# Identity from a count and a matmul, first two x tiles ahead of narrow weight columns, turned tiles split beside products: the first stage of an attention-and-experts kernel

## The chip, the core and the metric

The kernel runs on one core of one Trainium2 chip. The metric is the device time of one execution in microseconds; the span of a profiled execution is what its trace covers. Engine names are those of the profile: PE is TensorE (PEld its weight loads), DVE VectorE, ACT ScalarE, POOL GpSimd, SP SyncE (SPq its queue of DMA issues).

## What is computed

x is 2048 tokens of 512 features. All arithmetic is float32.

```python
xn = layernorm(x)                                   # over the 512 features, eps 1e-5
s  = latent attention(xn)                           # c_Q = xn W_DQ', c_KV = xn W_DKV', 16 heads of 128 + 64 rotary, causal
w  = top-2 of softmax(xn router_w') over 8 experts
g  = silu(xn weight' + 2 * sum_e w_e (xn A_e') B_e) # rank 16 per expert
return x + s * g
```

## The kernel before

Three programs run one after the other, each a block with a program for every engine: `prepare` (projections of the normalised tokens, to about 151 us of the trace), `attend` (scores, softmax and values, to about 1244 us) and `combine`. The change is in `prepare` alone, and in its first group.

`prepare` takes the 16 tiles of 128 tokens in four groups of four. For a tile, DVE works out mean and variance (L482, L486), ACT the root (L402), DVE the inverse and the normalised tile `xn` (L491, L497). PE turns `xn` by four transposes against the identity `ident` into PSUM (`turn_x`, L310; `turn_ps` has two banks, so a turn waits until DVE has used the tile two before it). ACT rounds it to the high half `xt_h` (L417) and DVE subtracts to get the low half `xt_l` (L504). A float32 product is made as three products of such halves, and the weights are split the same way: ACT `w_h` (L407), DVE `w_l` (L509). The four chunks `w_stage[:, c, :]` hold 128 of the 512 features each, with 1032 columns: 512 for the experts' base, then 128 for the low-rank factors, 8 for the router, 128, 128 and 128 for keys/values, queries and rotary keys.

For a group PE then makes, in this order: for each tile a product with 264 columns (L335, 12 matmuls; ACT copies part of it to `value_out`, L429, DVE takes two parts, L525 and L526; `work_ps` has two banks, so a product waits until DVE has read the one two before it); three products over the four tiles together (L345, 12 matmuls of 512 columns each; in the first group `absorb`, L298, stands after the first of them); the base product (L372, the first to use the 512 wide columns); and the low-rank part (L383 to L385). In the first group PE begins with four turns and nothing runs before all constants are there: PE and ACT wait for the semaphore `constants`, which POOL raises with its memsets and masks. POOL makes `ident` by a memset and an `affine_select`. All order is written out by hand, and every wait is a count on a semaphore.

## Time and profile before

| | us |
|---|---|
| median of 3 runs | 1454.61 (1453.51 to 1456.13) |
| the profiled execution | 1453.58 |
| its span | 1452.1 |
| PE busy | 1378.6 |
| DVE busy | 1141.7 |
| ACT busy | 781.3 |

The span is 1.5 us shorter than the time of the same execution. Busy times of the engines overlap. A timeline row gives the start, the duration from the first instruction's start to the last one's end, and in brackets how long the engine sat idle before it and what ended that.

### The profile page before, as it was taken

To read this page: it belongs to the slowest core of one execution; us is meant where nothing else is said; L and a number is where in the kernel's file an instruction comes from. 1 tells how busy PE (TensorE), PEld (TensorE's weight loads), DVE (VectorE), ACT (ScalarE), POOL (GpSimd) and SP (SyncE) were. 2 spreads that over 40 slices of the span, in tenths; PEclk is the share of its full clock that TensorE was granted. 3 is DMA by queue.
4 is the path that set the end of the run, shared out by engine and by line. 5 is a ranking of instruction groups with operands and counts; after the bars stand their busy time and mean duration, and the time that the engine had idled before them with its cause. 6 is when DMAs were issued, how large, how long until landed. Compare 5 with 4: busy or idle time off the path is not lost. (4 is left out here: it accounts for less than half of the span.)

```text
span 1452.1 us, 27828 instructions
## 1 busy us (share of the span) xinstructions
PE 1378.6 (95%) x9808; PEld 1133.0 (78%) x9808; DVE 1141.7 (79%) x1322; ACT 781.3 (54%) x854; POOL 112.6 (8%) x150
## 2 busy tenths in 40 slices
PE   5999689999999999999999999999999799599998
PEld 5888567778778888888889888887788688278887
DVE  5666378888888898989888898888788598576764
ACT  3322367666666666666666665666556466332221
POOL 0000111101101101010010100100000000112121
PEclk9999899999999999999999999999999999899999
DMA  6422665535424424242251421422412522345562
GB/s 265 134 90 85 187 187 153 168 130 157 120 89 148 123 85 124 84 126 83 58 152 58 123 87 61 136 74 56 129 54 83 189 57 58 117 132 161 167 181 87
DMA packets 111949, 172.77 MB, mean 119 GB/s; under 512 B 9224, under 2 KB 68904, under 8 KB 109096
## 3 DMA queue, kind: packets, MB, share of 16 engines
q1 hardware_dynamic: 97528, 111.10, 24.8%
q0 software_dynamic: 13552, 59.60, 14.0%
q10 hardware_dynamic: 832, 1.57, 0.5%
q8 instruction: 22, 0.36, 0.1%
q14 instruction: 15, 0.12, 0.0%
HBM read 123.75 MB, written 48.50 MB: 119 GB/s over the span
## 5 line engine op out<-in xcount | busy, mean ns | idle before, releaser
L1093 ACT CAST prob_h<-prob 128x1024 fp32r<-128x1024 f32 (+1 forms) x288 | 289.7, 1006 | 230.4 <-DVE prob L1177 183.1
L946 PE MATMUL score_ps<-q_h,key_slot 64*128 64x512 f32 x1792 | 360.8, 394 | 14.7 <-DMA key_slot<-keys 14.5
L1087 ACT ACTIVATE prob<-score_ps 128x1024 f32<-128x1024 f32 (+1 forms) x288 | 281.8, 978 | 168.0 <-PE score_ps L946 119.0
L1195 DVE TENSOR_TENSOR prob_l<-prob,prob_h 128x1024 fp32r<-128x1024 f32 (+1 forms) x288 | 335.9, 1166 | 39.7 <-ACT prob_h L1093 38.2
L968 PE MATMUL out_ps<-prob_h,value_slot 64*128 64x512 f32 (+1 forms) x1792 | 341.5, 375 | 0.2
L1190 DVE TENSOR_TENSOR total<-total,prob 128x1024 f32<-128x1024 f32 (+1 forms) x256 | 294.9, 1152 | 0.0
L1177 DVE TENSOR_SCALAR prob<-prob 128x1024 f32<-128x1024 f32 x224 | 155.2, 693 | 84.8 <-ACT prob L1087 84.6
L946 PEld LDWEIGHTS score_ps<-q_h,key_slot 64*128 64x128 f32 x1792 | 173.8, 185 | 52.8 <-DMA key_slot<-keys 10.8
L968 PEld LDWEIGHTS out_ps<-prob_h,value_slot 64*128 64x128 f32 x1792 | 173.7, 185 | 33.6 <-DVE prob_l L1195 2.3
L946 PE MATMUL score_ps<-q_l,key_slot 64*128 64x512 f32 x896 | 179.0, 391 | 0.0
L946 PE MATMUL score_ps<-rot_hh,key_slot 64*128 64x512 f32 x896 | 178.9, 390 | 0.0
L968 PE MATMUL out_ps<-prob_l,value_slot 64*128 64x512 f32 (+1 forms) x896 | 172.3, 376 | 0.0
L1391 ACT CAST rows_h<-rows 128x1024 fp32r<-128x1024 f32 x32 | 33.7, 1053 | 128.6 <-DVE rows L1423 127.2
L1376 PE MATMUL sum_ps<-merged_h,rows_h 128*128 128x512 f32 x256 | 100.0, 391 | 0.0
L946 PEld LDWEIGHTS score_ps<-rot_hh,key_slot 64*128 64x128 f32 x896 | 86.7, 184 | 16.9
L1378 PE MATMUL sum_ps<-merged_h,rows_l 128*128 128x512 f32 x256 | 99.6, 389 | 0.0
L1377 PE MATMUL sum_ps<-merged_l,rows_h 128*128 128x512 f32 x256 | 99.6, 389 | 0.0
L968 PEld LDWEIGHTS out_ps<-prob_l,value_slot 64*128 64x128 f32 x896 | 86.9, 185 | 16.1
L946 PEld LDWEIGHTS score_ps<-q_l,key_slot 64*128 64x128 f32 x896 | 86.8, 185 | 12.8
L946 PE MATMUL score_ps<-rot_l,key_slot 64*128 64x512 f32 x448 | 89.4, 390 | 0.0
L1182 DVE SCALAR_TENSOR_TENSOR prob<-prob,causal 128x1024 f32<-128x1024 f32 (+1 forms) x64 | 61.1, 954 | 17.3 <-ACT prob L1087 16.9
L1423 DVE TENSOR_TENSOR rows<-rows,scale 128x1024 f32<-128x1024 f32 x32 | 39.5, 1271 | 31.2 <-POOL scale L1358 31.2
(192 smaller groups left out, 1979.9 us busy)
## 6 DMA issues: line engine op xcount, KB each, us to landing
key_slot<-keys SPq DMA_DIRECT2D x144, 256.0 KB, 2.7
value_slot<-values SPq DMA_DIRECT2D x144, 128.0 KB, 2.0
rows<-heads_rows SPq DMA_DIRECT2D x32, 512.0 KB, 5.8
rot_hh<-turned POOLq DMA_DIRECT2D x30, 512.0 KB, 6.0
heads_rows<-head_rows POOLq DMA_DIRECT2D x15, 1024.0 KB, 10.0
turned<-rot_hl POOLq DMA_DIRECT2D x14, 1024.0 KB, 4.6
rot_l<-turned POOLq DMA_DIRECT2D x30, 256.0 KB, 7.9
wo<-in_w_o POOLq DMA_DIRECT2D x1, 4096.0 KB, 14.5
```

Of the source, the lines that this page charges most:

```text
L946: mm = pe.matmul(score_ps[:, half, c * 512:(c + 1) * 512], keys_of[ROWS[r], :], moving[par][ROWS[r], half * HW + c * 512:half * HW + (c + ...
L968: mm = pe.matmul(out, values_of[ROWS[r], :], moving, start=False, stop=False)
L1087: nc.scalar.activation(prob[half][:, 0:width], score_ps[:, half, 0:width], ACT.Exp, scale=QK_SCALE).then_inc(exp_done, 1)
L1093: nc.scalar.copy(prob_h[half][:, 0:width], prob[half][:, 0:width]).then_inc(high_done, 1)
L1177: nc.vector.tensor_scalar(p, p, P_MIN, P_MAX, ALU.max, ALU.min).then_inc(clipped, 1)
L1182: nc.vector.scalar_tensor_tensor(out=heads, in0=heads, scalar=P_MIN, in1=limit, op0=ALU.max, op1=ALU.min).then_inc(clipped, 1)
L1190: nc.vector.tensor_tensor(sums, sums, by_head(half, kind), ALU.add).then_inc(summed, 1)
L1195: nc.vector.tensor_tensor(p_l, p, p_h, ALU.subtract).then_inc(split, 1)
L1376: pe.matmul(sum_ps[:, par, :], rows_h[par][:, h, :], merged_h[:, h, :], start=(h == 0), stop=False)
L1377: pe.matmul(sum_ps[:, par, :], rows_h[par][:, h, :], merged_l[:, h, :], start=False, stop=False)
L1378: mm = pe.matmul(sum_ps[:, par, :], rows_l[par][:, h, :], merged_h[:, h, :], start=False, stop=(h == HEADS - 1))
L1423: nc.vector.tensor_tensor(rows[par][:, heads, :], rows[par][:, heads, :], scale[par][:, heads, :], ALU.mult).then_inc(scaled, 1)
```

## The change

- The identity is made otherwise. DVE writes the numbers 0 to 127 along the free dimension by one memset and seven additions, each on a result twice as wide; PE multiplies that by `share`, a tile of 1/128, which gives every partition its own number; DVE copies it out and compares. POOL's `affine_select` for `ident` goes.
- ACT waits for `eps` alone and PE for the steps of the identity; only DVE still waits for `constants`, behind its two normalisations.
- SP loads x tiles 0 and 1, then the narrow part of each weight chunk (520 columns), then x tiles 2 and 3, then the wide part (512 columns): four DMA issues more, ahead of the issues for `uq` and `uk`.
- Statistics, root, inverse and normalisation are done in pairs of tiles, with a statistic, a root and an inverse instruction for each tile.
- The turns of tiles 2 and 3 stand in PE's program behind the 264-column products of tiles 0 and 1, and their splits on ACT and DVE stand before the copies of those products.
- The wide halves are split behind the fourth product's copies, and PE waits for them before the base product.

```diff
-            for a in range(GROUP):
+            for a in range(2):
+                load_first(a)
             for c in range(KC):
-                sp.dma_start(w_stage[:, c, :], w_all[c * P:(c + 1) * P, :]).then_inc(w_in[c], 16)
+                sp.dma_start(w_stage[:, c, NARROW], w_all[c * P:(c + 1) * P, NARROW]).then_inc(w_in[c], 16)
+            for a in range(2, GROUP):
+                load_first(a)
+            for c in range(KC):
+                sp.dma_start(w_stage[:, c, WIDE], w_all[c * P:(c + 1) * P, WIDE]).then_inc(w_wide_in[c], 16)
...
-            nc.gpsimd.memset(ident[:, :], 0.0).then_inc(cleared, 1)
+            nc.gpsimd.memset(eps[:, :], EPS).then_inc(eps_set, 1)
+            nc.gpsimd.memset(share[:, :], 1.0 / P).then_inc(share_set, 1)
...
-            pe.wait_ge(constants, CONSTANTS)
+            pe.wait_ge(share_set, 1)
+            pe.wait_ge(counted, COUNTED)
+            pe.matmul(work_ps[:, 0, 0:EXPERTS], ident[:, :], share[:, :], start=True, stop=True).then_inc(placed, 1)
+            pe.wait_ge(ident_set, 1)
...
-            for a in range(GROUP):
+            for a in range(2):
                 turn_x(a, 0)
...
                     mm.then_inc(worked, 1)
+                    if first and a + 2 < GROUP:
+                        turn_x(a + 2, 0)
...
+                if first:
+                    pe.wait_ge(wide_low, KC)
...
-            act.wait_ge(constants, CONSTANTS)
+            act.wait_ge(eps_set, 1)
...
+            deviation_of(0)
+            deviation_of(1)
+            w_high_part(0)
+            w_high_part(1)
+            turn_x(0, 0)
+            turn_x(1, 0)
+            w_high_part(2)
+            w_high_part(3)
+            deviation_of(2)
+            deviation_of(3)
...
+            nc.vector.memset(ident[:, 0:1], 0.0).then_inc(counted, 1)
+            for n in range(COUNTED - 1):
+                dve.wait_ge(counted, n + 1)
+                nc.vector.tensor_scalar(ident[:, 2 ** n:2 ** (n + 1)], ident[:, 0:2 ** n], float(2 ** n), None,
+                                        ALU.add).then_inc(counted, 1)
...
+            dve.wait_ge(placed, 1)
+            nc.vector.tensor_copy(place[:, :], work_ps[:, 0, 0:1]).then_inc(place_read, 1)
+            dve.wait_ge(place_read, 1)
+            nc.vector.tensor_scalar(ident[:, :], ident[:, :], place[:, 0:1], None, ALU.is_equal).then_inc(ident_set, 1)
+            statistics_of(0)
+            statistics_of(1)
+            normalise_two(0)
```

PE's program from its start, before: the four turns (16 transposes), the first product (each weight chunk takes three matmuls), and where the third kind of product begins.

```order
L310 MATMUL turn_ps<-ident,xn 128x128 x16
L335 MATMUL work_ps<-w_h,xt_h 128x264
L335 MATMUL work_ps<-w_h,xt_l 128x264
L335 MATMUL work_ps<-w_l,xt_h 128x264
...
L345 MATMUL work_ps<-xt_h,w_h 128x512
```

And in the change, with the first product cut after its first chunk.

```order
L318 MATMUL work_ps<-share,ident 128x8
L326 MATMUL turn_ps<-ident,xn 128x128 x8
L351 MATMUL work_ps<-w_h,xt_h 128x264
L351 MATMUL work_ps<-w_h,xt_l 128x264
L351 MATMUL work_ps<-w_l,xt_h 128x264
...
L326 MATMUL turn_ps<-ident,xn 128x128 x4
L351 MATMUL work_ps<-w_h,xt_h 128x264
...
L326 MATMUL turn_ps<-ident,xn 128x128 x4
L351 MATMUL work_ps<-w_h,xt_h 128x264
```

Two of the four turns have moved behind the first and the second product.

DVE's program from its start to the first copy of a product, before.

```order
L482 BN_STATS stats<-x_all 128x6 x4
L484 REGISTER_ALU
L486 BN_AGGR moments<-stats 128x2 x4
L491 RECIPROCAL rstd<-deviation 128x4
L497 TENSOR_SCALAR xn<-x_all,moments,rstd 128x512 x4
L509 TENSOR_TENSOR w_l<-w_stage,w_h 128x1032 x2
L504 TENSOR_TENSOR xt_l<-turn_ps,xt_h 128x4x128
L509 TENSOR_TENSOR w_l<-w_stage,w_h 128x1032
L504 TENSOR_TENSOR xt_l<-turn_ps,xt_h 128x4x128
L509 TENSOR_TENSOR w_l<-w_stage,w_h 128x1032
L504 TENSOR_TENSOR xt_l<-turn_ps,xt_h 128x4x128 x2
L525 COPY small<-work_ps 128x136
```

And in the change, from the step behind the first normalised pair (the brackets name the semaphore waited for).

```order
L566 TENSOR_TENSOR w_l<-w_stage,w_h 128x520 [waits w_high] x2
L561 TENSOR_TENSOR xt_l<-turn_ps,xt_h 128x4x128 [waits turn_high] x2
L566 TENSOR_TENSOR w_l<-w_stage,w_h 128x520 [waits w_high] x2
L523 BN_STATS stats<-x_all 128x6 [waits x_first2]
L525 BN_AGGR moments<-stats 128x2 [waits first_stats]
L523 BN_STATS stats<-x_all 128x6 [waits x_first3]
L525 BN_AGGR moments<-stats 128x2 [waits first_stats]
L530 RECIPROCAL rstd<-deviation 128x1 [waits first_dev] x2
L554 TENSOR_SCALAR xn<-x_all,moments,rstd 128x512 [waits first_rstd] x2
L561 TENSOR_TENSOR xt_l<-turn_ps,xt_h 128x4x128 [waits turn_high,constants]
L597 COPY small<-work_ps 128x136 [waits work_high]
```

The statistics and the normalisation of tiles 2 and 3 now stand behind the narrow weight splits, and the split of turned tile 2 behind them.

## Rows read from the trace of the kernel before

**Rows 1.** Busy time in one stretch: PE, PEld, DVE, ACT, POOL, granted clock, DMA share, GB/s.

```profile
167.00:1244.00 1077.00, 1050.96 (x8272) 864.49 (x8271) 918.98 (x961) 676.01 (x700) 68.03 (x108) 0.99 0.36 108
```

**Rows 2.** Timeline, all engines, from the start to the first turn.

```profile
1.03 0.20 POOL L275 MEMSET ident<- 128x128 f32 x1 [0.29 <-POOLq L1526]
...
2.47 0.31 POOL L281 MEMSET cq_l<- 128x256 f32 x1
...
3.82 0.69 DVE L482 BATCH_NORM_STATS2 stats<-x_all 128x6 f32<-128x512 f32 x1 [3.82 <-DMA x_all<-in_x]
...
7.64 0.38 DVE L486 BATCH_NORM_AGGREGATE moments<-stats 128x2 f32<-128x6 f32 x4
...
11.64 0.20 ACT L411 ACTIVATE warm<-eps 128x1 f32<-128x1 f32 x1 [9.32 <-POOL ones L288]
11.75 0.28 ACT L402 ACTIVATE deviation<-moments,eps 128x4 f32<-128x4 f32 x1
...
12.27 1.92 DVE L497 TENSOR_SCALAR xn<-x_all,moments,rstd 128x512 f32<-128x512 f32 x4
...
12.96 1.09 PE L310 MATMUL turn_ps<-ident,xn 128*128 128x128 f32 x4 [12.96 <-DVE xn L497]
```

**Rows 3.** Timeline from the first weight split to the first product.

```profile
14.10 2.37 DVE L509 TENSOR_TENSOR w_l<-w_stage,w_h 128x1032 fp32r<-128x1032 f32 x2
...
18.13 0.68 DVE L504 TENSOR_TENSOR xt_l<-turn_ps,xt_h 128x512 fp32r<-128x512 f32 x1
18.35 0.58 ACT L417 CAST xt_h<-turn_ps 128x512 fp32r<-128x512 f32 x1 [1.28 <-PE turn_ps L310]
...
18.96 1.09 PE L310 MATMUL turn_ps<-ident,xn 128*128 128x128 f32 x4 [0.65 <-DVE xt_l L504]
...
19.70 0.57 PE L335 MATMUL work_ps<-w_h,xt_h 128*128 128x264 f32 x1
```

**Rows 4.** Timeline, products of the first group.

```profile
21.17 0.42 PE L335 MATMUL work_ps<-w_h,xt_h 128*128 128x264 f32 x1
...
21.39 0.42 PE L335 MATMUL work_ps<-w_h,xt_l 128*128 128x264 f32 x1
...
23.10 0.30 DVE L525 COPY small<-work_ps 128x136 f32<-128x136 f32 x1 [1.71 <-ACT value_out L429]
...
23.76 0.28 PE L335 MATMUL work_ps<-w_h,xt_h 128*128 128x264 f32 x1
...
23.88 0.28 PE L335 MATMUL work_ps<-w_h,xt_l 128*128 128x264 f32 x1
...
27.05 0.39 PE L345 MATMUL work_ps<-xt_h,w_h 128*128 128x512 f32 x1
```

**Rows 5.** Timeline, DVE and PE up to the base product.

```profile
31.79 0.19 DVE L549 TENSOR_TENSOR rt<-rt,order 128x32 f32<-128x32 f32 x1
...
32.01 0.19 DVE L550 TENSOR_REDUCE r<-rt 128x4 f32<-128x32 f32 x1
...
35.53 2.35 DVE L580 TENSOR_TENSOR absorb_l<-base_ps,absorb_h 128x1024 fp32r<-128x1024 f32 x2
...
38.99 0.39 PE L372 MATMUL base_ps<-w_h,xt_h 128*128 128x512 f32 x1
```

**Rows 6.** DMA issues: count, KB each, median us from issue to landing.

```profile
w_stage<-in_w_all SPq DMA_DIRECT2D x4, 516.0 KB, 6.8
...
x_all<-in_w_uk SPq DMA_DIRECT2D x1, 1024.0 KB, 11.6
```

**Rows 7.** Timeline of SP's queue.

```profile
5.56 0.44 SPq L227 DMA_DIRECT2D x_all<-in_w_uk  x1
```

**Rows 8.** Timeline of PE as the second program begins.

```profile
155.54 0.36 PE L881 MATMUL score_ps<-cq_h,absorb_h 128*128 128x256 f32 x1 [4.52 <-PEq L115]
...
155.85 0.29 PE L883 MATMUL score_ps<-cq_h,absorb_l 128*128 128x256 f32 x1
```

**Rows 9.** Waits of PE from 800 to 1200 us: total, times, longest.

```profile
PE score_ps L946 <- DMA key_slot<-keys: 8.2, 4, 6.2
```

More of the change, by code:

```diff
@@ L167, in prepare @@
         w_in = [sem(f"w_in{c}") for c in range(KC)]
+        w_wide_in = [sem(f"w_wide_in{c}") for c in range(KC)]
+        wide_high, wide_low = sem("wide_high"), sem("wide_low")
+        eps_set, ident_set = sem("eps_set"), sem("ident_set")
+        share_set, counted, placed, place_read = sem("share_set"), sem("counted"), sem("placed"), sem("place_read")
+        first_stats, first_var, first_dev, first_rstd = (sem(f"first_{n}") for n in ("stats", "var", "dev", "rstd"))
         uqk_in, rest_in, qr_in = sem("uqk_in"), sem("rest_in"), sem("qr_in")
@@ L281, in _ @@
                 nc.gpsimd.memset(t[:, SEQ:SEQ + CT], 0.0).then_inc(constants, 1)
-            pool.wait_ge(cleared, 2)
-            nc.gpsimd.affine_select(out=ident[:, :], in_=ident[:, :], compare_op=ALU.not_equal, fill=1.0,
-                                    base=0, pattern=[[-1, P]], channel_multiplier=1).then_inc(constants, 1)
+            pool.wait_ge(cleared, 1)
             nc.gpsimd.affine_select(out=keep.causal[:, :], in_=keep.causal[:, :], compare_op=ALU.is_ge, fill=0.0,
@@ L398, in deviations @@
             def deviations(g):
-                act.wait_ge(var_done, g + 1)
-                since(act, rstd_done, g)
+                act.wait_ge(var_done, g)
+                if isinstance(g, int) and g == 1:
+                    act.wait_ge(first_rstd, GROUP)
+                else:
+                    since(act, rstd_done, g - 1)
                 nc.scalar.activation(deviation[:, :], moments[:, :, 1], ACT.Sqrt,
@@ L406, in w_high_part, with wide_high_part, deviation_of @@
                 act.wait_ge(w_in[c], 16)
-                nc.scalar.copy(w_h[:, c, :], w_stage[:, c, :]).then_inc(w_high, 1)
-            act.wait_ge(constants, CONSTANTS)
+                nc.scalar.copy(w_h[:, c, NARROW], w_stage[:, c, NARROW]).then_inc(w_high, 1)
+            def wide_high_part(c):
+                act.wait_ge(w_wide_in[c], 16)
+                nc.scalar.copy(w_h[:, c, WIDE], w_stage[:, c, WIDE]).then_inc(wide_high, 1)
+            act.wait_ge(eps_set, 1)
             nc.scalar.activation(warm[:, :], eps[:, :], ACT.Sqrt)
-            deviations(0)
-            w_high_part(0)
+            def deviation_of(a):
+                act.wait_ge(first_var, a + 1)
+                nc.scalar.activation(deviation[:, a:a + 1], moments[:, a, 1:2], ACT.Sqrt,
+                                     bias=eps[:, 0:1]).then_inc(first_dev, 1)
             def turn_x(a, n):
@@ L418, in turn_x @@
                                turn_ps[:, a % 2, :].rearrange("p (c t) -> p c t", c=KC)).then_inc(turn_high, 1)
-            for a in range(GROUP):
-                if a < KC - 1:
-                    w_high_part(a + 1)
-                turn_x(a, 0)
+            deviation_of(0)
[8 more added lines that the diff above has]
+            deviation_of(3)
             def group(g, first=False, last=False):
@@ L427, in group @@
                 for a in range(GROUP):
+                    if first and a + 2 < GROUP:
+                        turn_x(a + 2, 0)
                     act.wait_ge(worked, WORK * g + a + 1)
                     nc.scalar.copy(value_out[:, a, 0:P], work_ps[:, a % 2, C_KV - C_A:SMALL]).then_inc(work_high, 1)
+                if first:
+                    for c in range(KC):
+                        wide_high_part(c)
                 since(act, keys_out, 16 * KEY_STORES * g)
@@ L508, in w_low_part, with wide_low_part @@
                 dve.wait_ge(w_high, c + 1)
-                nc.vector.tensor_tensor(w_l[:, c, :], w_stage[:, c, :], w_h[:, c, :], ALU.subtract).then_inc(w_low, 1)
-            statistics(0, first=True)
-            inverses(0)
-            for a in range(GROUP):
-                normalise(0, a)
-            w_low_part(0)
-            for a in range(GROUP):
-                if a < KC - 1:
-                    w_low_part(a + 1)
-                turn_x(a, 0)
+                nc.vector.tensor_tensor(w_l[:, c, NARROW], w_stage[:, c, NARROW], w_h[:, c, NARROW],
+                                        ALU.subtract).then_inc(w_low, 1)
+            def wide_low_part(c):
+                dve.wait_ge(wide_high, c + 1)
+                nc.vector.tensor_tensor(w_l[:, c, WIDE], w_stage[:, c, WIDE], w_h[:, c, WIDE],
+                                        ALU.subtract).then_inc(wide_low, 1)
+            dve.wait_ge(placed, 1)
[5 more added lines that the diff above has]
+            normalise_two(0)
+            w_low_part(0)
+            w_low_part(1)
+            turn_x(0, 0)
+            turn_x(1, 0)
+            w_low_part(2)
+            w_low_part(3)
+            statistics_of(2)
+            statistics_of(3)
+            normalise_two(2)
             dve.wait_ge(constants, CONSTANTS)
@@ L523, in group @@
                 for a in range(GROUP):
+                    if first and a + 2 < GROUP:
+                        turn_x(a + 2, 0)
                     dve.wait_ge(work_high, (WORK - 1) * g + a + 1)
@@ L527, in group @@
                                             value_out[:, a, 0:P], ALU.subtract).then_inc(work_used, 1)
+                if first:
+                    for c in range(KC):
+                        wide_low_part(c)
                 dve.wait_ge(work_high, (WORK - 1) * g + GROUP + 1)
```

28 lines of the change are left out of this document (21 added, 7 removed).

## Prediction

> **What bounds the kernel now.** I read the stretches first: from 167 to 1244 us PE is busy 1051 of 1077 us [rows 1]. PE has next to no room in the long middle, and the last program ends on PE's products too. So what PE saves before its dense work begins moves everything behind it forward, unless something with its own clock (a transfer on the way from the start) is then late. The change touches only the start, so I read the timeline of the first 40 us next.
>
> There PE stands still until 12.96 us. DVE has the four aggregates done about 8.0 (7.64 + 0.38), but ACT's first activation starts at 11.64, released by POOL's last constant; DVE normalises from 12.27 and the first turn runs at 12.96 [rows 2]. The turns then interleave with weight splits on DVE (1.18 us for each 1032-column chunk): the first product's matmul starts at 19.70 [rows 3]. From there PE is dense: products, then the first matmul of the 512-column kind (L345) at 27.05 [rows 4]. I take this matmul as the marker: all PE work behind it is the same in both kernels. The question is when it starts in the changed kernel.
>
> [...] The spacing halves near 22.6, about 3 us after the first product began.
>
> **The change, step by step.** Each step takes durations from rows of before; 0.05 us is added for a semaphore to DVE or ACT and 0.12 to PE (as 18.13 + 0.68 = 18.81 to the turn at 18.96).
>
> *Identity.* Engines start at 1.03 [rows 2]. DVE's memset and seven additions form a chain; the nearest rows are the router's dependent small steps, 0.22 us apart (31.79 to 32.01) [rows 5]. Eight are 1.8 us: 2.8 us. The 8-column matmul is in no trace; below it is about 0.3, above it a first product matmul of 0.57 [rows 3] or a set of four transposes of 1.09 [rows 2]; one matmul is nearest to the 0.57 row, I take 0.5: 3.3. The copy and the comparison are small steps, about 0.5 together: 3.9. Tile 0 lands at 3.82 now [rows 2], so the price is about 0.1 us, with bounds of 0 and 0.7.
>
> *First pair.* A statistic is 0.65, a single aggregate some 0.15 (four take 0.38): DVE is through both tiles at 5.5. A root 0.28 and an inverse (now 12.27 - 11.75 = 0.52 for both) bring 6.0; normalising is 0.48 a tile (1.92 for four), tile 0 ready at 6.5, DVE free at 7.0. Turn 0 starts at 6.6 instead of 12.96 [rows 2]. Its 1.09 us end at 7.7, ACT's 0.58 at 8.3; DVE has meanwhile split two narrow chunks (half of 1.18 and a little, 0.62 each) and subtracts turn 0 until 9.05 (0.68) [rows 3]. Product 0 starts at about 9.15 instead of 19.70.
>
> *Weights.* A 516 KB chunk lands 6.8 us after its issue (median) [rows 6]. The narrow chunks are a quarter MB each, as an x tile is, and take the places of x tiles 2 and 3 in the queue; chunks 0 and 1 should be there at about 6 and 7, when ACT asks for them. Chunks 2 and 3 are wanted at 9 and 9.5, x tiles 2 and 3 at 11 and 12, the wide parts not before 21.8. The last matrix `uk` is issued at 5.56 and lands 11.6 later, at 17.2 [rows 6, 7]; four issues more put it back by some 2 us at worst, to 19, against its use at 24.3. Transfers cost nothing here as long as they are not over 5 us late.
>
> *DVE decides the rest.* Product 0 needs chunks 2 and 3 split (to 11.0), 12 matmuls of 0.22, the last issued at 11.8. DVE goes on with two statistics (0.8 each, 12.5), root and inverse (13.1), normalised tile 2 at 13.5. So turn 2 starts at 13.65, and PE is idle between for 1.8 us. Product 1 follows at 14.4 (a turn holds PE 0.74: 18.96 to 19.70) [rows 3] and takes 2.64 at the lower level: 17.0. Turn 3: 17.75. If the level rises 3 to 3.6 us after product 1 begins, as it did behind the first product now, that is at about 18; product 2 then issues until 19.3. Product 3 needs turn 3's split on DVE (18.1, 18.8, 19.5) and behind it the copies of product 1 (about 0.4, [rows 4]): 19.9. It starts at 20.0, takes 12 x 0.12 = 1.45, and the marker comes at 21.6 instead of 27.05: **5.4 us earlier**. Turn 0 is 6.4 us earlier and product 0 10.5; 5 of these go back because DVE prepares tiles 2 and 3 late and one at a time.
>
> *Behind the marker.* Four wide splits stand in front of the key copy: ACT 22 to 24.0, DVE 22.5 to 25.0 (0.61 each). ACT's key copy, behind the first 512-column product, is done at about 24.9, so the key subtraction is put back by 0.1 us. What it delays on DVE ends with the absorbed split, which PE waits for before the base product: now 35.53 + 2.35 = 37.9 against 38.99 [rows 5], so 1.1 us cover it. The wait for `wide_low` ends at 25.0, 8 us before its user.
>
> *Sum.* The profiled execution took 1453.58 us (span 1452.1 and 1.5 around it): 1453.6 - 5.4 = 1448.2. It lies 1.0 below the median of 1454.61, so against the median the same gain is 1449.2, which I forecast. No change could be told from one under 0.2%, 2.9 us.
>
> **A rule weighed.** The doublings run from 1.05 to 2.8 us, just when POOL writes its constants (1.03 to 2.78) [rows 2]; DVE is idle there now, so no row shows the two together. [...] As a mechanism of this kernel: if every doubling waits for the memset then running, the chain ends at most 1.75 us later (all of POOL's memset time), the statistics begin at 5.6 and the marker at 23.3. The gain would be 3.6 us, 1451.0 against the median. That is rival C.
>
> **The rivals.**
> - *A, the forecast*: marker at 21.6, 1449.2. Half of it hangs on when the level rises; anything from 17.4 to 19.5 gives 21.2 to 21.7, because DVE's split of tile 3 holds product 3 anyway. Chance 0.45.
> - *B, the level rises early.* Product 0 runs 9.15 to 11.9 almost dense, which now it does not do before 19.7. If that already lifts PE, and the 1.8 us behind it do not drop it, turn 2 and product 1 run at the higher level and the marker comes at 19.6 to 20.6: gain 6.4 to 7.4, 1447.2 to 1448.2. For it: after 4.52 us of idling the matmul at 155.85 still takes 0.29, as those at the higher level do and not the 0.42 of the lower [rows 4, 8]. Against it: now the turns from 12.96 on did not lift it. [...] Chance 0.27.
> - *C, the start of DVE's chain is dearer* (the memsets above, a slow first matmul, weight chunk 1 half a microsecond late): gain 2.9 to 4.4, 1450.2 to 1451.7. DVE is serial from 3.9 to 14, so each tenth lost there reaches the marker whole. Chance 0.15.
> - *D, the change does not do what it says*: the earlier marker meets a wait with its own clock. The candidate is `uk`: `absorb` wants it at 24.4. If queueing narrower pieces brought it at 27 or later, less than 2.9 us would be left. All loads issued up to it are the same bytes, now landed by 17.2, which speaks against. 1451.7 to 1457.5, worked out as 1449.2 plus 2.5 to 8.3. Chance 0.08.
> - *E, slower*: `attend` waits on PE for keys, 8.2 us in four waits between 800 and 1200, the longest 6.2 [rows 9]. These are chance meetings of transfers. A shift could add such waits; it decides from 8.3 us more (5.4 + 2.9), that is two more of the longest, 1449.2 + 12.4 = 1461.6. The three runs of before lie within 2.6 us, so such a wait does not come and go by itself. Chance 0.05.
>
> **How the numbers follow.** A, B and C are faster by over 0.2%: 0.87. D is mostly within it: 0.08. E: 0.05. The range from B's 1446.4 (its 7.4, less the 0.8 by which a median may fall below) to C's 1451.7 holds a little over 8 in 10.
>
> **What would show it.** First activation on ACT near 2.3 instead of 11.64; the comparison done near 3.9; first turn at 6.6; first product at 9.2; an idle gap of PE of 1.8 us before turn 2 at 13.65, released by DVE's normalisation; marker at 21.6; the base product 11.9 us behind it as now; the second program's first matmul 5.4 before 155.54. Spacings of 0.12 before 17 us mean B, a comparison at 4.8 or later means C, PE idle before `absorb` means D. I am wrong if the distance from the marker to the end grows or shrinks by more than 1.5 us.

## The result, and the profile after

The changed kernel takes 1445.11 us (median of 8 runs, 1443.23 to 1449.71), the kernel before 1453.69 (8 runs, 1450.42 to 1456.13): ratio 0.9945, 95% interval 0.9934 to 0.9957. That is 8.6 us faster, where 5.4 were forecast. The forecast of 1449.2 was 4.1 too high, and 1445.11 lies 1.3 below its range. The execution that was profiled took 1443.91 us, 9.7 less than the profiled one of before (1453.58).

Timeline of the changed kernel from the start to the second half of the pair work, all engines; it answers to [rows 2].

```profile
1.28 1.94 DVE L518 TENSOR_SCALAR ident<-ident 128x1 f32<-128x1 f32 x7
1.35 0.33 POOL L295 MEMSET order<- 128x1 f32 x8
...
2.33 0.20 ACT L437 ACTIVATE warm<-eps 128x1 f32<-128x1 f32 x1
...
3.37 0.57 PE L318 MATMUL work_ps<-share,ident 128*128 128x8 f32 x2 [3.37 <-DVE ident L518]
3.98 0.16 DVE L575 COPY place<-work_ps 128x1 f32<-128x1 f32 x1 [0.75 <-PE work_ps L318]
4.17 0.29 DVE L577 TENSOR_SCALAR ident<-ident,place 128x128 f32<-128x128 f32 x1
...
6.51 0.98 DVE L554 TENSOR_SCALAR xn<-x_all,moments,rstd 128x512 f32<-128x512 f32 x2
7.19 1.94 PE L326 MATMUL turn_ps<-ident,xn 128*128 128x128 f32 x8 [3.25 <-DVE xn L554]
...
9.68 0.59 PE L351 MATMUL work_ps<-w_h,xt_h 128*128 128x264 f32 x1 [0.55 <-DVE xt_l L561]
```

The wait for POOL is gone. ACT's first activation runs at 2.33 instead of 11.64, the identity's comparison ends at 4.46, the first turn is at 7.19 instead of 12.96 and the first product at 9.68 instead of 19.70. POOL's first `affine_select` still starts only at 12.52 here; nothing of the start waits for it. The additions that make the identity don't all take the same time: those of 2, 16 and 32 columns in this execution, and below them the one of 16 columns in another execution of the same kernel (a2 in the table further down). Between the bars stand the busy time in us and the mean of one in ns.

```profile
L518 DVE TENSOR_SCALAR ident<-ident 128x2 f32<-128x2 f32 x1 | 0.5, 482 | 0.0
L518 DVE TENSOR_SCALAR ident<-ident 128x16 f32<-128x16 f32 x1 | 0.2, 243 | 0.0
...
L518 DVE TENSOR_SCALAR ident<-ident 128x32 f32<-128x32 f32 x1 | 0.2, 182 | 0.0
...
L518 DVE TENSOR_SCALAR ident<-ident 128x16 f32<-128x16 f32 x1 | 0.2, 176 | 0.0
```

The same view for PE behind the first product; it answers to [rows 4].

```profile
12.40 0.42 PE L351 MATMUL work_ps<-w_l,xt_h 128*128 128x264 f32 x1
...
14.33 0.66 PE L326 MATMUL turn_ps<-ident,xn 128*128 128x128 f32 x4 [1.50 <-DVE xn L554]
14.74 0.37 PE L351 MATMUL work_ps<-w_h,xt_h 128*128 128x264 f32 x1
14.95 0.28 PE L351 MATMUL work_ps<-w_h,xt_l 128*128 128x264 f32 x1
15.06 0.28 PE L351 MATMUL work_ps<-w_l,xt_h 128*128 128x264 f32 x1
...
20.33 0.39 PE L363 MATMUL work_ps<-xt_h,w_h 128*128 128x512 f32 x1
...
32.28 0.39 PE L392 MATMUL base_ps<-w_h,xt_h 128*128 128x512 f32 x1
```

PE idles 1.50 us, released by DVE's normalised tile 2, as the forecast says. But the matmuls behind the gap are 0.12 us apart, not 0.22. The two levels of PE, in the prediction (its "spacing" is the same thing), in the expectations ("clock level") and below, are these two spacings of the 264-column matmuls: 0.22 the lower, 0.12 the higher. The granted clock does not tell them apart: from 14.30 to 17.00 it is 1.00 here and 1.00 in the third execution (a3), whose matmuls are still 0.22 apart there. In this execution PE is at the higher level already. The marker (the first 512-column matmul) is at 20.33. The base product follows 11.95 behind it (before: 11.94), so the wide weight parts cost nothing.

PE where the second program begins and where it first waits for keys; the first row answers to [rows 8].

```profile
149.19 0.49 PE L956 MATMUL score_ps<-cq_h,absorb_h 128*128 128x256 f32 x1 [4.83 <-PEq L115]
160.09 0.77 PE L991 MATMUL score_ps<-q_h,key_slot 128*128 128x512 f32 x1 [6.29 <-DMA key_slot<-keys]
```

The long middle, in the stretch that answers to [rows 1], which begins 7 us and ends 10 us earlier here: PE is busy the same 1051 us.

```profile
160.00:1234.00 1074.00, 1050.90 (x8272) 860.31 (x8272) 918.70 (x961) 675.18 (x699) 68.04 (x108) 0.99 0.36 108
```

### The profile page after: what moved, and what is told of

The parts are those of the page before. It is cut to its first block and busy times, and to the rows that moved or that the text cites. A ratio compares the mean times of both kernels' runs of the same rounds, so it can differ in the third digit from the quotient of the medians.

```text
span 1442.4 us, 27855 instructions
## 1 busy us (share of the span) xinstructions
PE 1379.0 (96%) x9810; PEld 1128.1 (78%) x9810; DVE 1147.8 (80%) x1339; ACT 782.7 (54%) x861; POOL 111.6 (8%) x149
## 5 line engine op out<-in xcount | busy, mean ns | idle before, releaser
L1021 PE MATMUL score_ps<-q_h,key_slot 64*128 64x512 f32 x1792 | 359.7, 394 | 12.1 <-DMA key_slot<-keys 11.2
L1021 PEld LDWEIGHTS score_ps<-rot_hh,key_slot 64*128 64x128 f32 x896 | 86.2, 184 | 17.4
```

Source lines behind the costliest of these rows:

```text
L1021: mm = pe.matmul(score_ps[:, half, c * 512:(c + 1) * 512], keys_of[ROWS[r], :], moving[par][ROWS[r], half * HW + c * 512:half * HW + (c + ...
```

## The experiments

All the kernels in one table. "Marker" and "second program" are the starts of those matmuls in the profiled execution, "rest" is that execution's time less the start of the second program, "mask" the start of POOL's first `affine_select`. Where a kernel has one execution alone, its time stands as "single", without a ratio.

| kernel | mask | marker | second program | rest | median us (runs) | ratio to before, 95% |
|---|---|---|---|---|---|---|
| before | 10.88 | 27.05 | 155.54 | 1298.0 | 1453.69 (8) | 1 |
| b1, b2, b3: before | 12.63, 11.27, 12.18 | 29.18, 28.37, 28.50 | 157.67, 156.90, 157.02 | 1295.4, 1295.9, 1297.1 | single: 1453.06, 1452.75, 1454.13 | |
| after | 12.52 | 20.33 | 149.19 | 1294.7 | 1445.11 (8) | 0.9945 (0.9934 to 0.9957) |
| a2: after | 11.76 | 20.52 | 149.21 | 1293.7 | 1443.82 (6) | 0.9938 (0.9919 to 0.9957) |
| a3, a4: after | 12.07, 11.80 | 21.90, 22.38 | 150.74, 151.08 | 1294.4, 1294.9 | single: 1445.17, 1445.96 | |
| e1, identity alone | 11.44 | 23.02 | 151.45 | 1290.9 | 1445.52 (6) | 0.9943 (0.9923 to 0.9964) |
| e9, the same again | 13.77 | 23.12 | 151.59 | 1294.1 | 1445.69 (5) | 0.9947 (0.9934 to 0.9961) |
| e8, e1 but waiting | 13.40 | 31.34 | 159.79 | 1292.3 | 1454.18 (11) | 1.0007 (0.9998 to 1.0016) |
| e2, old identity | 11.87 | 25.36 | 154.01 | 1294.6 | 1447.73 (4) | 0.9960 (0.9945 to 0.9976) |
| e3, turns first | 11.32 | 22.41 | 151.06 | 1296.5 | 1448.08 (6) | 0.9964 (0.9951 to 0.9977) |
| e7, old loads | 12.42 | 24.66 | 153.15 | 1294.8 | 1447.87 (6) | 0.9959 (0.9946 to 0.9971) |
| e4, warm | 13.45 | 20.34 | 149.06 | 1295.2 | 1445.39 (6) | 0.9948 (0.9930 to 0.9967) |
| e5, short product | 11.76 | 22.18 | 150.85 | 1294.2 | 1444.41 (5) | 0.9939 (0.9919 to 0.9960) |
| e6, one base twice | 11.71 | 22.05 | 153.47 | 1292.5 | 1447.27 (12) | 0.9966 (0.9952 to 0.9979) |
| e10, mask placed first | 9.81 | 27.75 | 156.26 | 1295.2 | single: 1451.41 | |
| f1, unused tiles | 12.92 | 30.07 | 158.51 | 1298.1 | 1454.01 (12) | 1.0009 (0.9997 to 1.0021) |
| f2, nine memsets | 11.73 | 28.06 | 156.50 | 1294.7 | 1451.53 (12) | 0.9986 (0.9972 to 0.9999) |

**The identity alone.** Before with the new identity and the narrower waits of PE and ACT; loads, order and turns are the old ones.

```diff
             pe.wait_ge(share_set, 1)
             pe.wait_ge(counted, COUNTED)
+            pe.matmul(work_ps[:, 0, 0:EXPERTS], ident[:, :], share[:, :], start=True, stop=True).then_inc(placed, 1)
+            pe.wait_ge(ident_set, 1)
...
-            act.wait_ge(constants, CONSTANTS)
+            act.wait_ge(eps_set, 1)
...
```

> The kernel before with the new identity and ACT waiting for eps alone; loads, splits and turns in the old order. Both theories have DVE normalise from about 8.6 instead of 12.27 (the fourth x tile lands at 6.8), but the first whole weight chunks land at 8.5 and 9.8 and stand on ACT ahead of the turn copies, so the first 512-column product of the first group starts at about 23.9 instead of 27.05. Theory 1 (all that PE saves ahead of this marker reaches the end one to one, the rest is scatter between runs): the time falls by 3.1 us, 2.5 to 4. Theory 2 (an earlier start also removes 2 to 3 us of waits for key transfers in the second program): it falls by 5 or more.

It ran at 0.9943 of before, 7.8 us faster by medians of all its comparison runs: by the time alone not to be told from the whole change. In the trace it can be: marker 23.02, where 23.9 was expected. The time fell by far more than the 3.1 us of the first theory. The rest of this execution, 1290.9, is the shortest of all, so the same kernel was measured again.

> The new identity alone once more, the kernel of the first experiment unchanged, for more runs and a second trace. There the marker (first 512-column product of the first group) was 4.0 us earlier and the time 7.8 lower. If the excess of 4 is scatter of six runs: 3.5 to 6 faster than before now. If it belongs to the kernel: 7 to 8.5 again, with the second program some 3 us or more shorter than before's in the trace.

Ratio 0.9947, marker 23.12, rest 1294.1. The identity brings most of the gain in the marker and, as far as the time can tell, all of it. The rest of 1290.9 did not come again, but 1294.1 is still 2.5 shorter than the mean of the four traces of before (1296.6).

**The identity, but the constants waited for as well.** The same kernel with the old wait put back beside the new ones.

```diff
             pe.wait_ge(ident_set, 1)
+            pe.wait_ge(constants, CONSTANTS)
...
             act.wait_ge(eps_set, 1)
+            act.wait_ge(constants, CONSTANTS)
```

> The new identity, but PE's turns and ACT's first root wait for all constants as before, so the first group starts as late as in the kernel before (marker 26.5 to 27.5). Theory 1 (one to one): no difference from before beyond 1 us. Theory 2 (something that the new identity's code carries with it, whatever the start, shortens the second program): 3 to 4 us faster than before. Theory 3 (an earlier start shortens it): as theory 1.

Timeline of this kernel, POOL and ACT behind the wait.

```profile
13.40 0.39 POOL L288 TENSOR_SCALAR_AFFINE_SELECT causal<-causal 128x256 f32<-128x256 f32 x1 [10.65 <-issue]
...
13.95 1.28 ACT L418 ACT_TABLE_LOAD   x1 [13.95 <-POOL ones L290]
15.24 0.20 ACT L418 ACTIVATE warm<-eps 128x1 f32<-128x1 f32 x1
```

The gain is gone (1.0007). So it is not the way the identity is made but what is no longer waited for. The marker is later even than before's: the mask came late in this execution (13.40), and the activation table's load of 1.28 us now stands behind the wait. That is a side effect of this experiment: with one wait ahead of the activation, as in before, the load ran at 1.03, and with two it ran at 13.95. So this kernel starts about 1.3 us later than a control should. Its time is that of before all the same: from the marker to the end it takes 1420.8 us, less than any of the four traces of before (1423.9 to 1426.5). The stretch behind the marker can be short without an early start.

**All but the identity.** The changed kernel with POOL's old identity; ACT's wait for `eps` alone stays, and PE waits for the identity and no other constant.

```diff
-            nc.gpsimd.memset(share[:, :], 1.0 / P).then_inc(share_set, 1)
+            nc.gpsimd.memset(ident[:, :], 0.0).then_inc(cleared, 1)
...
+            nc.gpsimd.affine_select(out=ident[:, :], in_=ident[:, :], compare_op=ALU.not_equal, fill=1.0,
+                                    base=0, pattern=[[-1, P]], channel_multiplier=1).then_inc(ident_set, 1)
...
```

> The changed kernel with the identity made by POOL's memset and affine_select again (about 11.2 to 12.9 us in the traces); loads, splits and turns as changed, statistics and roots early. The first turn waits for it: 11.3 to 13 instead of 7.2, and DVE's chain behind it is put back as much: marker 24.2 to 26. One to one this is 1 to 3 us faster than before: the order of work alone brings little as long as the identity is late.

Ratio 0.9960, some 5.8 us faster than before; 1 to 3 were expected. The marker, 25.36, is where it was expected (24.2 to 26), so what was missed lies behind it. The first turn waits for the mask here (12.21, where before it was 12.96), but the product follows only 2.5 us behind it, at 14.72 instead of 19.70, since normalised tiles and two weight chunks are ready by then.

**All four turns ahead of the products** (the two turns are put back to the head of PE's, ACT's and DVE's programs; loads and identity are new).

```diff
-            for a in range(2):
+            for a in range(GROUP):
                 turn_x(a, 0)
...
-                    if first and a + 2 < GROUP:
-                        turn_x(a + 2, 0)
...
```

> The changed kernel with the turns of tiles 2 and 3 and their splits ahead of all four products, on PE, ACT and DVE. PE is idle from 9 to 14.3 and makes four products behind 15.8, most of the first two at the lower clock level: marker at 22.5 to 23.2, 2.2 to 2.8 us later than in the changed kernel with the early clock and 0.5 to 1 with the late one. If products between the turns do not matter: 20.3.

Ratio 0.9964; the first product is at 15.95 instead of 9.68, the marker at 22.41. That is as late as the latest marker of the changed kernel itself (22.38, below), and its time is 3 to 4 us above that kernel's medians; how much of it is the order of the turns one trace doesn't show.

**The old loads** (four x tiles, then whole chunks of 1032 columns).

```diff
-                sp.dma_start(w_stage[:, c, NARROW], w_all[c * P:(c + 1) * P, NARROW]).then_inc(w_in[c], 16)
+                sp.dma_start(w_stage[:, c, :], w_all[c * P:(c + 1) * P, :]).then_inc(w_in[c], 16)
...
```

> The changed kernel with the loads of before: four x tiles, then whole weight chunks; the splits stay narrow first. Whole chunks land at 8.5, 9.8, 11.1 and 12.3, and two narrow casts stand on ACT ahead of the first turn's, so that turn's split moves from 8.3 to 10.4 and DVE's chain with it: marker 2 to 2.5 later than the changed kernel's with the same clock, 22.4 to 24.3. If the order of loads does not matter: 20.3 to 22.1, the two values seen for the changed code.

Timeline of this kernel, ACT's weight halves and the first product.

```profile
8.89 0.62 ACT L425 CAST w_h<-w_stage 128x520 fp32r<-128x520 f32 x1 [2.49 <-DMA w_stage<-in_w_all]
10.15 0.62 ACT L425 CAST w_h<-w_stage 128x520 fp32r<-128x520 f32 x1 [0.63 <-DMA w_stage<-in_w_all]
...
12.16 0.59 PE L347 MATMUL work_ps<-w_h,xt_h 128*128 128x264 f32 x1 [3.03 <-DVE xt_l L557]
```

Ratio 0.9959. The chunks are late by the trace's own word (2.49 us of waiting for the first), and what is split behind them is late by as much: the product at 12.16 instead of 9.68, turn 2 at 16.69 instead of 14.33, the marker at 24.66, a little later than expected.

**Is DVE's chain the bound?** Six more multiplications of `ident` ahead of the turns (two rows each in the trace), into a bank that nothing reads, so that the level rises early.

```diff
             pe.wait_ge(ident_set, 1)
+            for _ in range(6):
+                pe.matmul(base_ps[:, 0, 0:P], ident[:, :], ident[:, :], start=True, stop=True)
```

> The changed kernel with six extra float32 128x128 matmuls on PE behind the comparison, in the wait for the first normalised tile (about 4.5 to 7.2 us). If DVE's chain alone sets the marker, it stays at 20.3. If the clock level in the first turns and product 0 matters too, the turns run at the higher level, each turn reaches ACT 0.4 earlier, and the marker comes at 19.6 to 20.0. Time 0 to 0.7 us below the changed kernel, too small to tell by the time; the trace decides.

Timeline of PE of this kernel.

```profile
4.51 2.93 PE L321 MATMUL base_ps<-ident 128*128 128x128 f32 x12 [0.57 <-DVE ident L579]
...
9.69 0.39 PE L353 MATMUL work_ps<-w_h,xt_h 128*128 128x264 f32 x1 [0.55 <-DVE xt_l L563]
9.92 0.28 PE L353 MATMUL work_ps<-w_h,xt_l 128*128 128x264 f32 x1
...
14.34 0.66 PE L328 MATMUL turn_ps<-ident,xn 128*128 128x128 f32 x4 [1.95 <-DVE xn L556]
...
20.34 0.39 PE L365 MATMUL work_ps<-xt_h,w_h 128*128 128x512 f32 x1
```

The first product runs wholly at the higher level and ends earlier, and turn 2 starts at 14.34 all the same: PE only idles longer (1.95). Marker and time are those of the changed kernel's first execution. Up to turn 2 DVE decides. Behind it the level does: further executions of the changed kernel (below) have markers up to 22.38, so early warming may be worth something on average; with one trace of it that is not shown.

**The first product cut to its last chunk** (9 of the 12 matmuls of tile 0's first product are left out), to see whether that product lifts the level.

```diff
                     for c in range(KC):
+                        if first and a == 0 and c < KC - 1:
+                            continue
```

> The changed kernel with 9 of the 12 matmuls of tile 0's first product left out, so PE does a quarter of the work before the 1.5 us of idling; tile 0's small values are then not the reference's. Theory 1 (product 0's dense work lifts the clock before turn 2, which gave the marker at 20.33 and not 21.6): turn 2 and product 1 run at 0.22 a matmul and the marker comes at 21.3 to 22. Rival (the level rises then whatever PE does): marker unchanged at 20.3.

Turn 2 stayed at 14.33; the spacing halved behind product 1 and the marker came at 22.18. That looked like proof that product 0 lifts the level, until two further executions (below) showed the same late marker in the changed kernel itself. The time, 1444.41, shows no loss. Inconclusive.

**Does every microsecond reach the end?** Tile 0's base product of the first group (12 matmuls, 2.8 us) is made twice; the start is unaltered.

```diff
+                    for again in range(2 if first and a == 0 else 1):
```

> The changed kernel with the base product of tile 0 in the first group done twice: 12 matmuls of 0.23, 2.8 us more of PE work behind the marker. Theory 1 (one to one): 2.8 us slower than the changed kernel, so about 5.2 to 5.8 faster than before. Theory 2 (phase of the second program's transfers decides some waits): 4.5 to 5.5 slower than the changed kernel, or under 1.

1447.27 against 1445.11: 2.2 us for 2.8 put in; by the ratios, which compare each with executions of before beside it, 3.1 (0.9966 against 0.9945, with intervals that overlap). Both agree with time in the first program reaching the end whole, neither measures it to better than a microsecond or two.

**How steady is the kernel before?** Three more executions of it, unaltered.

> The kernel before, unchanged, for a second trace. In ten traces so far POOL's first affine_select starts between 10.9 and 13.8 us, and before's was the earliest of them; PE and ACT of before wait for it. Theory 4 (the trace that I predicted from had a luckily short wait for the constants): affine_select at 11.5 to 14 here and the marker (L345) as much later than 27.05, at 27.7 to 30. If before is always early: 10.9 and 27.05 again.

> As the run ahead of it, a third trace of before: by theory 4 the marker moves with the start of affine_select one to one (27.05 - 10.88 = 16.2 behind it, give or take 1 for the clock); if the excess of the measured gain is all in the second program, the marker stays at 27 and the stretch from the second program's first matmul to the end is 1298 us, against 1292 to 1296 in the traces of the other kernels.

> A fourth trace of the kernel before, with the same two expectations as the third: a marker that moves with affine_select by theory 4, or one that stays at 27 with a long second program.

Timeline of the first of these, POOL and ACT at the start; it answers to [rows 2].

```profile
12.63 0.28 POOL L283 TENSOR_SCALAR_AFFINE_SELECT ident<-ident 128x128 f32<-128x128 f32 x1 [9.85 <-issue]
...
13.39 0.20 ACT L411 ACTIVATE warm<-eps 128x1 f32<-128x1 f32 x1 [11.08 <-POOL ones L288]
```

POOL waits before its first `affine_select`, for nothing that the profile shows, and not equally long: 8.10 us in the trace that was read, then 9.85, 8.48 and 9.39. The first product follows the start of that `affine_select` by 8.8 us each time (19.70, 21.46, 20.09, 21.00). The marker is at 27.05, 29.18, 28.37 and 28.50; the trace on which the prediction rests had the luckiest start of the four.

**The mask placed first.** If POOL's wait belonged to the place, the mask would come early when it stands right behind two memsets. It is taken away where it stood.

```diff
             nc.gpsimd.memset(keep.causal[:, :], P_MAX).then_inc(cleared, 1)
+            pool.wait_ge(cleared, 2)
+            nc.gpsimd.affine_select(out=ident[:, :], in_=ident[:, :], compare_op=ALU.not_equal, fill=1.0,
+                                    base=0, pattern=[[-1, P]], channel_multiplier=1).then_inc(constants, 1)
```

> The kernel before with the identity's affine_select ahead of POOL's other memsets, so POOL asks for it at about 1.5 us and not 2.8. If the wait ahead of it (8.1 to 9.9 us in four traces of before) is a fixed piece of work: affine_select at 9.6 to 11.4. If it ends with something that starts with the program, whatever POOL did before: 10.9 to 12.7 as now, and the idle time before it 1.3 longer.

Timeline of POOL of this kernel.

```profile
1.18 0.32 POOL L276 MEMSET causal<- 128x256 f32 x1
9.81 0.28 POOL L278 TENSOR_SCALAR_AFFINE_SELECT ident<-ident 128x128 f32<-128x128 f32 x1 [8.32 <-issue]
```

It waits 8.32 us here too, with two memsets done, and starts at 9.81, as expected of a wait that goes with the instruction and not with the program's start. This is one execution. What the wait is for the profile does not say. The change takes it off the path by not needing the instruction.

**Where do 2 us behind the first program come from?** Before has a rest of 1296.6 (mean of four traces), the changed kernel 1294.4 (four), and all but e3 of the other kernels traced before these two 1295.2 or less. Two kernels of before with a side effect of the change alone: the new tiles and semaphores unused (f1), and these with nine small memsets on DVE at the start (f2, the last three lines).

```diff
+        share = sb("share", [P, EXPERTS])
+        place = sb("place", [P, 1])
+        eps_set, ident_set = sem("eps_set"), sem("ident_set")
+        share_set, counted, placed, place_read = sem("share_set"), sem("counted"), sem("placed"), sem("place_read")
...
+            for n in range(8):
+                nc.vector.memset(share[:, n:n + 1], 0.0)
+            nc.vector.memset(place[:, :], 0.0)
```

> The kernel before with the two small tiles and six semaphores of the change allocated and not used; no instruction differs. If the shorter second program comes with where tiles and semaphores lie: about 2.6 us faster than before, and PE's waits for key and rotary transfers between 170 and 400 us at 5.0 us or less (5.8 to 7.8 in four traces of before). If not: no difference from before (within 1 us).

> The same with nine small memsets on DVE at the program's start, in its idle time ahead of the first x tile, so every later instruction of DVE lies nine places further. If the second program's length hangs on where its instructions lie: about 2.6 us faster than before, or another clear difference. If not: none (within 1 us), marker 27 to 29.2.

f1 is no different from before (1.0009), its rest 1298.1. f2 took 0.9986, with a rest of 1294.7 but an interval that all but touches 1. Tiles and semaphores are ruled out; a small effect of what DVE does at the start is not, and e10's one execution, which has none of it, has a rest of 1295.2 too.

Part of the difference can be placed: a single wait of PE for keys late in the second program, the longest of that stretch. Timeline of PE there: before, the changed kernel, f1, f2, and the kernel with the new identity that waits (e8).

```profile
1140.32 0.80 PE L946 MATMUL score_ps<-q_h,key_slot 64*128 64x512 f32 x2 [6.23 <-DMA key_slot<-keys]
...
1131.29 0.80 PE L1021 MATMUL score_ps<-q_h,key_slot 64*128 64x512 f32 x2 [4.63 <-DMA key_slot<-keys]
...
1143.60 0.80 PE L950 MATMUL score_ps<-q_h,key_slot 64*128 64x512 f32 x2 [6.20 <-DMA key_slot<-keys]
...
1138.15 0.80 PE L953 MATMUL score_ps<-q_h,key_slot 64*128 64x512 f32 x2 [4.65 <-DMA key_slot<-keys]
...
1140.30 0.79 PE L963 MATMUL score_ps<-q_h,key_slot 64*128 64x512 f32 x2 [4.89 <-DMA key_slot<-keys]
```

It is 5.78 to 6.23 in the four traces of before and 4.63 to 5.18 in the four of the changed kernel: 1.1 us by the means. An early start is not what shortens it: it is short in f2 and e8, which start as late as before or later, and long in e3 (5.95) and e6 (5.75), which start early. What does is not known.

**How steady is the changed kernel?** Three more profiled executions, the first with timed runs beside it.

> The changed kernel again. The marker has been 20.33 and 20.34 with an early clock and 22.05 in a kernel with the same start and a late one: one of these two values here, to 0.2 us. Time 7 to 9 us below before, median 1444.5 to 1446.5.

> The changed kernel, unaltered. If the early rise of the level (rival B) is what the changed start does, the spacing of product 1 is 0.12 from its first matmul and the marker comes at 20.3 to 20.6, as in both traces so far. If the moment only scatters between executions, the marker can come at 21.6 to 22.2, as with the same start code and a longer base product behind it (22.05).

> As for the look before it: marker at 20.3 to 20.6 where the changed start itself lifts the level early, 21.6 to 22.2 in some executions where the moment scatters.

Timeline of PE of the last one, behind the first product.

```profile
14.33 1.11 PE L326 MATMUL turn_ps<-ident,xn 128*128 128x128 f32 x4 [1.51 <-DVE xn L554]
15.10 0.57 PE L351 MATMUL work_ps<-w_h,xt_h 128*128 128x264 f32 x1
15.46 0.42 PE L351 MATMUL work_ps<-w_h,xt_l 128*128 128x264 f32 x1
...
18.92 0.28 PE L351 MATMUL work_ps<-w_h,xt_l 128*128 128x264 f32 x1
...
22.38 0.39 PE L363 MATMUL work_ps<-xt_h,w_h 128*128 128x512 f32 x1
```

Turn 2 starts at the same 14.33, but product 1 keeps the spacing of 0.22 and only product 2 has 0.12. The markers are 20.33, 20.52, 21.90 and 22.38: in two executions the level had risen by turn 2, in two between 17.7 and 18.9. The first of the three has a median of 1443.82, a little below what was expected. The code is the same in all four, so it isn't the code. The two late ones ran on one chip and the second early one on another, so a difference between chips is not ruled out; in what follows the moment is called a draw.

## Why the prediction was wrong in size and right in kind

Two steps of the sum 1453.6 - 5.4 failed: the stretch behind the marker, which it took as unchanged, and the marker of before, which it took from one execution. The miss of 4.1 us, by what moved, with means over four traces of each kernel:

- 0.9: the base. The forecast starts from a median of 1454.61 over 3 runs; over 8 runs it is 1453.69.
- 1.2: **a step that failed.** "ACT's first activation starts at 11.64, released by POOL's last constant" was read off one execution, and with it the 27.05 from which the gain is counted. Four traces have the marker at 28.28 on average (27.05 to 29.18). The wait that the change removes is a scattering one, and the trace at hand had its shortest.
- 0.3: the marker of the changed kernel, 21.28 on average (20.33 to 22.38), for a forecast of 21.6.
- 1.9: behind the marker. From it to the end the kernel before takes 1425.1, the changed one 1423.2. **This is the largest step that failed**: "all PE work behind it is the same in both kernels" holds for the work, but the sum took the time as the same too and put nothing on a change there. Without it the time would be 1447.0, inside the range; without the 1.2 it would be 1446.3, still just outside. The prediction named a change of more than 1.5 there as what would make it wrong, and that happened. The four of before lie between 1423.9 and 1426.5, the four of the changed kernel between 1422.4 and 1423.6. The cause is open, see below.

These sum to 4.4 before rounding; that the profiled executions stand a little otherwise to the medians takes 0.3 back.

Point by point:

- *What bounds the kernel.* Right. The base product made twice added 2.2 (by medians) to 3.1 us (by ratios) for 2.8 put in, and PE's busy time in the middle is the same to 0.1 us.
- *Identity.* Its comparison was forecast done at 3.9 and ends at 4.46. The additions, taken at 0.22 from one to the next, are that far apart only at the end, where POOL's memsets are over (2.75): the ones of 32 and 64 columns start at 2.81 and 3.03. Beside the memsets they are 0.27 apart, and once 0.52 (see rivals C to E, below); that is 0.5 us of the chain. The 8-column matmul runs in 0.57 as the nearest row says. Together DVE starts 0.6 us later than forecast, within the bounds of 0 to 0.7.
- *First pair.* Turn 0 at 7.19 for 6.6, product 0 at 9.68 for 9.15: both late by that 0.6, not by more.
- *Weights.* Right: a narrow chunk lands in time, the wide parts and `uk` are waited for nowhere. With the old loads the marker is at 24.66, so this part is worth 2.3 to 4.3 us in the marker against the changed kernel's four (one trace with the old loads).
- *DVE decides the rest.* Right up to turn 2: the gap before it is 1.50 for 1.8, released by `xn`, and warming PE early doesn't move it. Behind it the level counts for more than the forecast had: rises between 17.4 and 19.5 were to give 21.2 to 21.7, and the two late executions have 21.90 and 22.38. The 3 to 3.6 us from a product's first matmul to the rise were an estimate from the one trace read (19.70 to 22.71, 3.0); the other three of before have 3.9, 5.0 and 3.2, so no fixed time is shown. Product 1 at the lower level holds PE 2.8 us (15.10 to 17.88 in a4), where the sum has 2.64.
- *Rival A or B.* Both levels occur, each in two of four executions. Where the level rises early the marker is at 20.33 and 20.52 (B's 19.6 to 20.6), where it rises between 17.7 and 18.9 at 21.90 and 22.38 (A's 21.6, with the excess just named). The forecast treated as a question of the code what is a draw. What sets the moment the traces don't show: behind the eight transposes of turns 0 and 1 (from 7.19, in a2 from 7.37) product 0 had the spacing of 0.22 in all four executions, and with six more multiplications (2.93 us) ahead of the same transposes 0.12 (e4); but product 0 itself is 2.7 us of matmuls and kept the 0.22 to its end as well. The level's moment is worth 1.4 to 2.1 us in a trace, but it is not what put the time below the range.
- *Behind the marker.* Right for the first program: the base product 11.95 behind it, and to the second program 128.51 before and 128.78 after. The 2.2 us come after that. PE's waits for keys between 800 and 1200 us are 8.2 in [rows 9] and 6.7 to 8.2 in the four traces of before, 6.3 to 6.9 in the four of after; by the means that is 1.0 of it, and the one wait shown above (6.05 against 4.93 by the means) makes up all of that. Another 0.5 lies where the third program's products wait for `merged_l` (12.5 against 12.1 by the means, with ranges that overlap). Where the remainder lies was not followed up. Why the long wait is shorter isn't settled: it is no matter of tiles or semaphores (f1) nor of the early start (f2 and e8, e3 and e6). **Open.** The prediction did look at these waits, but only as rival E, which had them grow and took them for chance meetings of transfers. That was the author's estimate: the long one stands in every one of the eight traces.
- *Rivals C to E.* None came as priced, but C's mechanism is there, at about a third of its price. POOL's memsets and DVE's additions ran together until 2.75. The additions of 2, 4, 8 and 16 columns took 0.48, 0.24, 0.24 and 0.24 us; those of 32 and 64, wider but behind the last memset, 0.18 and 0.20. In execution a2 the chain ran later and the addition of 16 columns, too, started behind the last memset (2.78 against 2.72): it took 0.18 there. The memsets took up to 0.33, against 0.31 alone [rows 2]. So the two do slow each other: seven additions took 1.94, against the 1.5 forecast, and 2.12 in a2, where the one of 2 columns took 0.73; that is also why turn 2 and the marker are 0.2 later in a2 than in the first execution. The bound, every addition waiting for the memset then running, is not what the rows show: a memset ran from 2.42 to 2.75 and an addition beside it from 2.54 to 2.78. The price is 0.5 to 0.7 us and not the 1.75 of the bound.

What is the gain made of? The marker moves from 28.28 to 21.28, 7.0 us. The identity with its waits gives 5.2 of them (to 23.07, two traces), all the other edits without it 2.9 (25.36, one trace). Their sum is 8.1, so they overlap by 1.1; the narrower waits of ACT and PE are in both. In the time the identity alone is at 0.9943 and 0.9947, the whole at 0.9945 and 0.9938: the 1.8 us that separate the markers are about what these measurements can resolve. That the other edits add anything on top of the identity is shown by the traces and not by the times.

## What to carry to other kernels

Where a gain is the removal of a wait "for issue", look at more than one execution of the kernel before: a wait with no named cause has its own scatter, and the sum inherits it (here 1.2 of the 8.6 us). Where a sum takes the long stretch behind the change as unchanged, give that a width of its own: here it moved by 1.9 us, more than any other term missed, and four traces of one kernel alone lie 2.6 apart in it. Split a constant's wait by who needs what: one slow instruction behind a shared count held ACT for 9.3 us here, and DVE and PE behind it, and the cure was to leave it off the path, not to place it earlier. Keep a chain of small DVE instructions clear of POOL's memsets where it can be had: beside them a step cost 0.27 us and more, alone 0.22. Where the spacing of PE's matmuls falls in mid-start (here from 0.22 to 0.12 us), treat its moment as a draw with both outcomes in the range, and ask which engine would bind next before spending work on warming PE.

## What the runs showed of the hardware

- The first `affine_select` of POOL starts 9.81 to 13.77 us into the trace in every kernel traced, after 8.1 to 11.0 us of "issue", with 2 or with 15 of the kernel's memsets ahead of it. Where another stands right behind it, that one starts 0.26 us later (10.88 and 11.14 in before).
- Additions of DVE on 2 to 16 columns took 0.24 to 0.73 us while POOL's memsets ran, and 0.18 to 0.20 on 16 to 64 columns behind them (12 traces of kernels with the new identity).
- A POOL `affine_select` of 128x256 took 0.39 us while DVE was idle (before, 11.14) or at statistics (after, 12.52). Where it started while DVE was at its subtractions `w_l` it took 1.66 and 1.31 us (identity alone, two traces) and 0.63 (turns first), each time ending 0.25 us behind the last such subtraction, and DVE's own durations stayed (2.37 for two). Started 0.1 us before the end of one, it took 0.39 (a2). So it is POOL's instruction that was longer there, not DVE's; in the identity's first trace a subtraction began after it (11.62) and ended ahead of it (12.85 against 13.10). Timeline of the identity alone:

```profile
10.47 2.37 DVE L520 TENSOR_TENSOR w_l<-w_stage,w_h 128x1032 fp32r<-128x1032 f32 x2
...
11.44 1.66 POOL L288 TENSOR_SCALAR_AFFINE_SELECT causal<-causal 128x256 f32<-128x256 f32 x1 [8.69 <-issue]
```

- An activation table load of 1.28 us ran at 1.03 with one semaphore wait written ahead of ACT's first activation (before), and at 13.95, behind the waits, with two (e8).
- PE's 264-column matmuls were 0.12 us apart from turn 2 on (14.33 and 14.51, whose four transposes took 0.66 for 1.12 and 1.11 in the others) in two executions of one and the same kernel, and came to 0.12 only between 17.7 and 18.9 in two others, with the same PE work to within 0.2 us until turn 2. With six more multiplications ahead of the turns the first product's were 0.12 apart, from 9.92 on.
